# A graph network layer on one core: programs of their own for the closing steps, the final pair's gates as plain products, its mixing on VectorE

## The reference

```
mask   = (adj[None] == labels)                       # 4 labels
weight = mask / (sum(mask, -1) + EPS)
agg    = einsum('dbmn,bnh->bmdh', weight, hid)       # mean over neighbours, per label
out    = relu(agg @ Wd.T + bd)
r = sigmoid(out @ Wri.T + bri + hid @ Wrh.T + brh)
z = sigmoid(out @ Wzi.T + bzi + hid @ Wzh.T + bzh)
n = tanh(out @ Wni.T + bni + r * (hid @ Wnh.T + bnh))
out = (1 - z) * n + z * hid
out = (out - mean(out)) / sqrt(var(out) + LN_EPS) * gamma + beta
```

## Time and profile before

| what | value |
|---|---|
| median of 3 runs | 548.65 us (547.62 to 548.74) |
| the profiled execution | 547.88 us, of which the span from first to last instruction 546.1 us |
| PE busy | 512.1 us, 94% of the span |
| PEld busy | 467.4 us, 86% |
| DVE busy | 436.0 us, 80% |
| ACT busy | 387.9 us, 71% |
| POOL busy | 301.4 us, 55% |
| mean granted clock of TensorE | 0.976 of 2.4 GHz |

### The profile page before, as it was taken

How to read it: one execution, slowest core, us unless ns; L and a number is a source line. 1 busy time by engine, 2 the same in 40 slices (tenths; PEclk the granted TensorE clock), 3 DMA queues, 4 the chain that set the end, 5 groups by cost and what they waited for, 6 DMA issues and landing times.

```text
span 546.1 us, 10515 instructions
## 1 busy us (share of the span) xinstructions
PE 512.1 (94%) x3011; PEld 467.4 (86%) x3011; DVE 436.0 (80%) x1075; ACT 387.9 (71%) x725; POOL 301.4 (55%) x311
## 2 busy tenths in 40 slices
PE   4759999999999999999999999999999999999970
PEld 2548999999999999999999999999999999999860
DVE  5685688888888888888888888888888888888755
ACT  4366777777777777777777777777777777777651
POOL 5564555655565556556655566565555665653333
PEclk9688999999999999999999999999999999999996
DMA  8302022122111221222111211121112122110100
GB/s 283 111 30 68 1 68 69 49 69 68 68 50 39 67 67 48 67 67 67 51 36 67 67 48 67 67 67 56 35 63 67 49 66 67 38 38 29 40 31 38
DMA packets 19877, 33.42 MB, mean 61 GB/s; under 512 B 2224, under 2 KB 6576, under 8 KB 19856
## 3 DMA queue, kind: packets, MB, share of 16 engines
q1 hardware_dynamic: 19728, 32.78, 18.4%
q0 software_dynamic: 128, 0.39, 0.2%
HBM read 24.77 MB, written 8.39 MB: 61 GB/s over the span
## 4 chain that ended last, share of the span: by engine, by line
PE 88%; issue 3%; POOL 3%; DVE 3%; ACT 2%; DMA 1%; SPq 0%; POOLq 0%; DVEq 0%; ACTq 0%
PE y_bank L281 33%; PE alpha L281 23%; PE gamma L281 11%; PE p_bank L344 11%; PE beta L281 6%; PE t_bank L383 2%; DMA shared<-in_wdT 1%; PE t_bank L325 1%; DVE masks L645 1%; DVE y_lo L592 0%; POOL shared L840 0%; POOL shared L845 0%; POOL x_lo L827 0%; ACT y_hi L448 0%; ACT x_hi L495 0%
## 5 line engine op out<-in xcount | busy, mean ns | idle before, releaser
L827 POOL TENSOR_TENSOR x_lo<-x_f,x_hi 128x1024 fp32r<-128x1024 f32 x31 | 80.9, 2611 | 102.0 <-ACT x_hi L495 102.0
L448 ACT ACTIVATE y_hi<-y_bank 128x512 fp32r<-128x512 f32 x128 | 76.8, 600 | 63.7 <-PE y_bank L281 63.6
L281 PE MATMUL y_bank<-wd_hi,x_hi 128*128 128x512 f32 x256 | 106.1, 414 | 4.7 <-DVE wd_lo L580 4.7
L281 PE MATMUL y_bank<-wd_lo,x_hi 128*128 128x512 f32 x256 | 103.6, 405 | 0.0
L281 PE MATMUL y_bank<-wd_hi,x_lo 128*128 128x512 f32 x256 | 103.1, 403 | 0.0
L592 DVE TENSOR_TENSOR y_lo<-y_bank,y_hi 128x512 fp32r<-128x512 f32 x128 | 86.9, 679 | 13.9 <-ACT y_hi L448 13.8
L344 PE MATMUL p_bank<-y_hi,masks 128*128 128x256 f32 x256 | 68.0, 287 | 9.6 <-DVE y_lo L592 8.6
L864 POOL TENSOR_TENSOR o_lo<-o_sums,o_hi 128x512 fp32r<-128x512 f32 x32 | 41.4, 1295 | 52.8 <-ACT o_hi L547 52.8
L344 PE MATMUL p_bank<-y_lo,masks 128*128 128x256 f32 x256 | 67.6, 286 | 0.0
L456 ACT ACTIVATE p_bank<-p_bank,ratio 128x256 f32<-128x256 f32 x128 | 52.5, 456 | 11.0 <-PE p_bank L344 11.0
L281 PEld LDWEIGHTS y_bank<-wd_hi,x_hi 128*128 128x128 f32 x256 | 49.9, 195 | 12.0 <-issue 5.5
(11 more groups left out here) (116 smaller groups left out, 1357.2 us busy)
## 6 DMA issues: line engine op xcount, KB each, us to landing
x_f<-in_xT SPq DMA_DIRECT2D x32, 256.0 KB, 2.6
x_rows<-in_x SPq DMA_DIRECT2D x32, 256.0 KB, 3.0
out<-shared SPq DMA_DIRECT2D x32, 256.0 KB, 2.0
adj_in<-in_adjT SPq DMA_DIRECT2D x31, 128.0 KB, 2.4
shared<-in_wgT SPq DMA_DIRECT2D x2, 576.0 KB, 7.4
shared<-in_wdT SPq DMA_DIRECT2D x3, 256.0 KB, 6.4
vec_rows<-in_vectors SPq DMA_DIRECT2D x1, 512.0 KB, 8.4
x_rows<-in_vectors SPq DMA_DIRECT2D x1, 512.0 KB, 10.0
```

Of the source, the lines that this page charges most:

```text
L281: done = nc.tensor.matmul(dst, m, w, start=(first and t == 0), stop=(last and t == 2), skip_group_check=inside)
L448: nc.scalar.activation(y_hi[:, g, half(b)], y_bank[b][:, :], ACT.Copy)\
L827: nc.gpsimd.tensor_tensor(*split_lo(x_lo[:, k % XRING, :, :], x_f[:, k % 2, :, :], x_hi[:, k % XRING, :, :])).then_inc(xlo_ready, 1)
```

## The change

The steps 32 to 35 are replaced by a function `tail()` on each engine, written out for pairs 29 to 31 (`run_steps` now ends before step 32).

- The final pair's gates are eight plain products (no sums of `x` or `o`): each of four banks (`y_bank0`, `y_bank1`, `p_bank`, `beta`) collects one 128-node by two-gate block of one graph; ACT writes the bias into it first (`seed`), the `x` halves come early and the `o` halves when `o_lo` is there. The graph with index 1 (`ODD`) comes first.
- Its sigmoids are taken bank by bank, its hidden part and sum in pieces of 128 columns, its mixing `x - n`, `z *`, `+ n` on DVE for each graph, its statistics and normalization for each graph with stores of their own.
- Pair 30 keeps the seven products; pairs 29 and 30 are normalized by ACT (scaling with `rstd`) and POOL (addition of beta) in place of DVE. On SP the store of pair 30 stands ahead of the two stores of pair 31.
- PE's transposes of pair 31 come after the product S2,T2 in place of before it; the relu of `o` is done once for the whole bank.
- The plain products need block `B12` of the weights, split in step 3, and a bias `half_bias`, made on POOL in step 3. `n_sb` lies elsewhere in `shared`, so that `B12` stays whole until then.

The parts of the diff in the steps, whole:

```
-WBLOCKS = 7
+WBLOCKS = 8
-ASKED = (B11, T1, T2, B21, T3, T4, B22)
+ASKED = (B11, T1, T2, B21, T3, T4, B22, B12)
-        n_sb = later(4608, 1)
+        n_sb = later(7168, 1)
-            for i in range(LAST, STEPS):
+            for i in range(LAST, PAIRS):
                 step(i, lambda n, k=1: n)
...
@@ ACT, after u3 and ahead of o_hi of the sums
                 if i == 2:
                     weights_o(B22)
+                if i == 3:
+                    weights_x(B12)
+                    weights_o(B12)
...
@@ POOL, after x_lo and ahead of the mixing
                 if i == 2:
                     for w in (B21, T3, T4, B22):
                         weights_o(w)
+                if i == 3:
+                    weights_o(B12)
+                    nc.gpsimd.tensor_tensor(half_bias[:, :], vec_rows[:, 0:512], bias_step[:, :], ALU.add)\
+                        .then_inc(half_bias_ready, 1)
                 if has_pair(m):
                     pool.wait_ge(tanh_ready, up(m + 1))
```

The tail programs, cut to their order:

```
+    # SP
+    def tail():
+        rows(PAIRS - 2)
+        sp.wait_ge(result_ready, 2 * (PAIRS - 3))
+        store(PAIRS - 4)
+        rows(PAIRS - 1)
+        sp.wait_ge(late_ready, 1)
+        store(PAIRS - 3)
+        sp.wait_ge(late_ready, 2)
+        store(PAIRS - 2)
+        for n, g in ((1, ODD), (2, EVEN)):
+            sp.wait_ge(end_ready, n)
+            sp.dma_start(out[PAIRS - 1][:, g * H:(g + 1) * H], end_out[:, g, :]).then_inc(stored[1], 16)
+    # PE (waits for operands left out)
+        product(alpha, A11, B11).then_inc(p1_done, 1)
+        (second label sums of graph 1)
+        product(gamma, S1, T1).then_inc(p5_done, 1)
+        product(alpha, S2, T2).then_inc(p6_done, 1)
+        (transposes)
+        product(beta, A12, B21).then_inc(p2_done, 1)
+        product(alpha, S3, T3).then_inc(p7_done, 1)
+        from_x((ODD, 0))
+        product(alpha, A22, T4).then_inc(p4_done, 1)
+        from_x((ODD, 1))
+        product(gamma, S4, B22).then_inc(p3_done, 1)
+        from_o((ODD, 0))
+        from_x((EVEN, 0))
+        from_o((ODD, 1))
+        from_x((EVEN, 1)).then_inc(x_gates_done, 1)
+        from_o((EVEN, 0))
+        pe.wait_ge(end_nh_ready, 1)
+        from_o((EVEN, 1))
+    # ACT, from the sigmoid of pair 30
+        sigmoid(last - 1)
+        end_gate((ODD, 0), end_r_ready)
+        end_gate((ODD, 1), end_z_ready)
+        tanh(last - 1)
+        scale_norm(last - 2, 0)
+        end_tanh(ODD, 2)
+        act.wait_ge(x_gates_done, 1)
+        nc.scalar.activation(end_nh[:, :], beta[:, 0:128], ACT.Copy).then_inc(end_nh_ready, 1)
+        end_gate((EVEN, 0), end_r_ready)
+        end_tanh(EVEN, 4)
+        end_gate((EVEN, 1), end_z_ready)
+        scale_norm(last - 1, 2)
+    # DVE, from the c12 sum of pair 30
+        moments(last - 2)
+        hidden(last - 1, gamma)
+        centre(last - 2, 0)
+        centre(last - 2, 1)
+        end_hidden(ODD, 0, 1, y_bank[0][:, 0:128])
+        end_sum(ODD, 0, 1)
+        end_hidden(ODD, 1, 1, y_bank[1][:, 0:128])
+        end_sum(ODD, 1, 2)
+        end_hidden(EVEN, 0, 2, p_bank[:, 0:128])
+        end_sum(EVEN, 0, 3)
+        end_hidden(EVEN, 1, 2, end_nh[:, :])
+        end_mixed(ODD, 1)
+        end_sum(EVEN, 1, 4)
+        end_moments(ODD, 1)
+        mixed(last - 1)
+        end_mixed(EVEN, 2)
+        end_centre(ODD, 1)
+        end_moments(EVEN, 2)
+        end_normal(ODD, 1)
+        moments(last - 1)
+        end_centre(EVEN, 2)
+        end_normal(EVEN, 2)
+        centre(last - 1, 0)
+        centre(last - 1, 1)
+    # POOL
+        mixing(last - 2)
+        root(last - 2)
+        mixing(last - 1)
+        add_beta(last - 2, 1)
+        end_root(ODD, 1)
+        end_root(EVEN, 2)
+        root(last - 1)
+        add_beta(last - 1, 2)
```

More of the change, by code:

```diff
@@ L17 @@
 LAST = FIRST + ROUNDS * BODY
+ODD, EVEN = 1, 0
 GATE = 3 * 128
@@ L100, in gnn_kernel @@
         normed = later(6144, 2).rearrange("p (k g f) -> p k g f", k=2, g=2)
+        sides = lambda t: t.rearrange("p (g f) -> p g f", g=2)
+        scratch = x_f[:, :, :, :].rearrange("p k b n -> p (k b n)")
+        end_rz = scratch[:, 0:1024].rearrange("p (g j f) -> p g j f", g=2, j=2)
+        end_pre = sides(scratch[:, 1024:1536])
+        end_out = sides(scratch[:, 1536:2048])
+        end_rn = out_rows
+        end_part = sides(o_sums[:, 0:4, :].rearrange("p b n -> p (b n)"))
+        end_stats = sb("end_stats", [128, 2, 6])
+        end_mv = sb("end_mv", [128, 2, 2])
+        end_rstd = sb("end_rstd", [128, 2])
+        end_nh = sb("end_nh", [128, 128])
+        half_bias = sb("half_bias", [128, 512])
         more_vec = x_rows[:, :, :, :].rearrange("p k g f -> p (k g f)")
@@ L111, in gnn_kernel @@
         mix = bank("mix")
+        gate_bank = {(ODD, 0): y_bank[0], (ODD, 1): y_bank[1], (EVEN, 0): p_bank, (EVEN, 1): beta}
+        end_n, end_d, end_mix = sides(alpha[:, :]), sides(gamma[:, :]), sides(t_bank[:, :])
         x_loaded = [sem("x_loaded0"), sem("x_loaded1")]
@@ L192, in gnn_kernel @@
         scaled_ready = sem("scaled_ready")
+        half_bias_ready = sem("half_bias_ready")
+        seeded = {key: sem(f"seeded_{key[0]}{key[1]}") for key in gate_bank}
+        gates_done = {key: sem(f"gates_done_{key[0]}{key[1]}") for key in gate_bank}
+        x_gates_done = sem("x_gates_done")
+        end_nh_ready = sem("end_nh_ready")
+        end_r_ready = sem("end_r_ready")
+        end_z_ready = sem("end_z_ready")
+        end_rn_ready = sem("end_rn_ready")
+        end_pre_ready = sem("end_pre_ready")
+        end_n_ready = sem("end_n_ready")
+        end_d_ready = sem("end_d_ready")
+        end_part_ready = sem("end_part_ready")
+        end_mix_ready = sem("end_mix_ready")
+        end_stats_ready = sem("end_stats_ready")
+        end_mv_ready = sem("end_mv_ready")
+        end_ve_ready = sem("end_ve_ready")
+        end_rstd_ready = sem("end_rstd_ready")
+        end_centred = sem("end_centred")
+        end_ready = sem("end_ready")
+        late_scaled = sem("late_scaled")
+        late_ready = sem("late_ready")
         result_ready = sem("result_ready")
@@ L269, in step, with rows, store @@
                         .then_inc(stored[j % 2], 16)
+            def rows(k):
+                sp.wait_ge(from_ready, k - 1)
+                sp.dma_start(x_rows[:, k % 2, :, :], x[k].rearrange("p (g f) -> p g f", g=2))\
+                    .then_inc(rows_loaded[k % 2], 16)
+            def store(j):
+                sp.dma_start(out[j].rearrange("p (g f) -> p g f", g=2), normed[:, j % 2, :, :]).then_inc(stored[j % 2], 16)
+            def tail():
[10 more added lines that the diff above has]
+                    sp.dma_start(out[PAIRS - 1][:, g * H:(g + 1) * H], end_out[:, g, :]).then_inc(stored[1], 16)
             run_steps(sp, step)
-            for slot in range(2):
-                sp.wait_ge(stored[slot], 16 * PAIRS // 2)
+            tail()
+            sp.wait_ge(stored[0], 16 * PAIRS // 2)
+            sp.wait_ge(stored[1], 16 * PAIRS // 2 + 16)
         @block.tensor
@@ L409, in step, with tail, product, from_x @@
                     count(i + 1)
+            def tail():
+                q, last, slot = PAIRS - 2, PAIRS - 1, (PAIRS - 1) % XRING
+                def product(dst, left, w):
+                    three_passes(dst[:, 0:GATE], x_hi[:, q % XRING, left, :], x_lo[:, q % XRING, left, :],
+                                 wx_hi[:, w, :], wx_lo[:, w, :])
+                    return three_passes(dst[:, 128:512], o_hi[:, q % 2, left - 1, :], o_lo[:, q % 2, left - 1, :],
+                                        wo_hi[:, w, :], wo_lo[:, w, :])
+                inner = {(ODD, 0): ((A11, B11), (A12, B21)), (ODD, 1): ((A11, B12), (A12, B22)),
+                         (EVEN, 0): ((A21, B11), (A22, B21)), (EVEN, 1): ((A21, B12), (A22, B22))}
+                o_place = {A21: 3, A22: 0, A11: 1, A12: 2}
+                def from_x(key):
+                    pe.wait_ge(seeded[key], 1)
+                    for left, w in inner[key]:
+                        done = three_passes(gate_bank[key][:, 0:GATE], x_hi[:, slot, left, :], x_lo[:, slot, left, :],
+                                            wx_hi[:, w, :], wx_lo[:, w, :])
+                    return done
+                def from_o(key):
+                    for left, w in inner[key]:
+                        at = o_place[left]
+                        done = three_passes(gate_bank[key][:, 128:512], o_hi[:, last % 2, at, :],
+                                            o_lo[:, last % 2, at, :], wo_hi[:, w, :], wo_lo[:, w, :])
+                    done.then_inc(gates_done[key], 1)
+                pe.wait_ge(alpha_loaded, PAIRS - 1)
+                pe.wait_ge(olo_ready, PAIRS - 1)
+                product(alpha, A11, B11).then_inc(p1_done, 1)
+                pe.wait_ge(p_scaled, 4 * PAIRS)
+                for b in range(2):
+                    d = 2 * b + 1
+                    for part in (y_hi, y_lo):
```

(31 more changed lines are left out.)

207 lines of the change are left out of this document (added).

## The result

The changed kernel takes 554.45 us (median of 4 runs, 553.79 to 555.07) against 548.65 before: ratio 1.011, 95% interval 1.0092 to 1.0128. Forecast were 553.6 and 551.2 to 555.7. The profiled execution has a span of 552.0 us.

A forecast was written before the change was run, and what follows sets the result against it. PE was taken as the bound except at the two ends, where any delay from step 3 on is paid in full; front 8.9 less tail 3.9 gave +5.0, on the median 553.6 us, range 551.2 to 555.7.

The forecast's parts named there:

- The front's order: Step 3: POOL waits 4.6 us for ACT's wo_hi ahead of the mixing, which starts 6.94 late.
- From DVE to PE: Step 3: DVE's late mix add delays c22, PE idles 6.0 us; y_lo then makes the P matmuls 7.0 late.
- The clock: After the 6.0 us gap PE returns at granted clock 0.50, making the next product 8.9 us late, not 7.0.
- The tail: Closing steps: the new order ends the program 3.9 us earlier, bounds 2.5 to 4.9.
- The walk itself: Step-by-step timing of the tail: c12 of pair 30 at 522.3, DVE ending at 536.65, the span at 542.2.
- The named weakness: Tail: SP stores pair 30 first, so ACT's scalings (0.81) and POOL's addition (1.3) precede the three stores.
- The clock did not stay high: Rival, 10%: the clock stays high after PE's gap; front 7.0, tail 3.9, so +3.1, 551.8 us.
- The front was not hidden: Rival, 6%: POOL's wait in step 3 costs nothing and only the tail's gain is left, 544.7 us.
- The tail did not give nothing: Rival, 5%: DVE's smaller pieces and pair 30 stored first cancel the tail's gain; 8.9 alone, 557.5 us.
- A stall of some 3.9: Rival, 2%: a partly hidden stall of about 3.9 us would give no change.

The follow-up runs named there:

- e1: The changed kernel with POOL's split of B12 and half_bias moved from ahead of the mixing to behind rstd in step 3: 545.67 us, ratio 0.9954.
- e4: The changed kernel with ACT's two splits of B12 moved up to the start of step 3, POOL's order kept: 549.40 us, ratio 1.0029.
- e3: The changed kernel with 30 matmuls of zeros on PE in step 3, between A22,T4 and the wait for c22: 553.11 us, ratio 1.009.
- e5: e1 with POOL's addition of beta for pair 29 moved behind the root of the odd graph in the tail: 545.46 us, ratio 0.9939.
- e6: e5 with pair 30's moments, centrings and root ahead of the last pair's closing operations, and its store last: 542.82 us, ratio 0.9892.
- e7: e6 with DVE's split of B12 moved from ahead of the c22 sum to the end of step 3: 542.87 us, ratio 0.99.
- e8: The changed kernel with POOL's o_lo of step 3 made to wait for DVE's mix add of pair 0: 554.81 us, ratio 1.012.
- e2: The kernel before with only the change's step 3 insertions (B12 split, half_bias, unread) and the old closing steps: 557.41 us, ratio 1.016.

## Why the prediction was right, point by point

**The front's order: right.** POOL's wait was 4.66 (forecast 4.6), its releaser ACT's wo_hi; the mixing started 6.9 late (73.79, against 67.61 less the head's 0.71). e1 and e4 show that both the wait and the 2.3 us of work behind it count.

**From DVE to PE: one term missing.** The sum had the mix add at 0.70. It took 1.74 beside POOL's o_lo, and PE's gap was 6.9 where 6.0 were forecast. The step that failed is "z_part comes 6.9 late, and the rest follows with the durations of before": POOL's o_lo came late as well and landed on the add.

**The clock: the mechanism right, its size too large.** PE came back at 0.50. The low clock lasted 4.6 us after the return (79.89 to about 84.5), not the 5.8 of the earlier trace rows, and cost 1.2 us (e3) where 1.9 stood in the sum (8.9 less 7.0). The two errors, +1.04 and -0.7, nearly cancel: forecast 8.9, measured 9.2. That the front fits is partly luck.

**The tail: right in kind, 1.3 us too good.** 2.6 where 3.9 were forecast. Of the missing, 0.92 is the product of end_nh, 1.20 in place of 0.28 (e5 gives 0.84 of it back); the sigmoid of pair 30 starts 0.54 after the c12 sum ends (530.75 to 531.29), where the sum had nearly nothing. The walk itself held: the c12 sum ends at 530.75, forecast 522.3 plus the shift of 8.48, 530.8; from DVE's last operation to the end 5.46, forecast 5.55. The last matmul ends 3.2 sooner on the shifted scale (537.9 less 8.48, against 532.6), not 4: PE's wait for end_nh was 1.30 where the sum had 0.7, off the deciding path as forecast. The named weakness, pair 30's store ahead of the last pair's, is real: e6 takes 2.0 us out of it.

**The total.** By the traces both ends together are +6.6 (9.19 less 2.58) where +5.0 stood in the sum, and nearly all of the difference is the tail's. The profile's head was 0.71 shorter by chance, and the medians differ by 5.8. The forecast of 553.6 is 0.85 below the 554.45 measured, inside the stated range.

**The rivals.** The clock did not stay high. The front was not hidden. The tail did not give nothing. A stall of some 3.9 did not occur: PE's gap was 6.90.

## What to carry to other kernels

An insertion into an in-order engine costs what stands behind it, not its busy time: 2.3 us of work with a wait of 4.7 ahead of a chain that had no slack cost PE 9 us once, and the same work behind that chain under 1. Before placing a one-time preparation, look for the instruction that another engine already waits for and go behind it. Then look what the work pushes back in turn: an operation that moves in time can land beside one of another engine that it slows (e7, e8). In a closing sequence, let the engine that runs without a gap finish last, with the shortest path from it to the store.

## What the runs showed of the hardware

DVE's TENSOR_TENSOR operations whose two inputs both lie in SBUF stood still while a POOL instruction that had started first ran: 1.74 us in place of 0.70 beside 1.26 of POOL, 1.20 in place of 0.28, 1.31 in place of 0.54. Operations with one input in PSUM did not (in e5 the sum of o_sums and alpha at 535.00 took 0.43 in the middle of POOL's addition of beta, 534.75 to 536.01). Taking the overlap away restored both durations (e5, e8). The Trainium skill, SBUF — State Buffer, section "Who interferes with whom", says that a DVE instruction with two SBUF inputs contends with a GpSimd instruction that reads SBUF; the trace agrees, with the numbers above. It goes the other way too: POOL's addition of one column, which started just behind DVE's mix add (540.78 and 540.62), took 0.59 us, and 0.19 where no such operation ran; the mix add kept its 0.70.

Two inputs in SBUF are not the only case. The masks of e7 have one, and four of them took 1.71 beside POOL in place of 0.90. And the trace of the kernel before had the effect already, in a small operation. The ratios of the counts (L621, 128x4, both inputs in SBUF) took (shortest, median and longest, in ns):

```profile
L621 DVE TENSOR_TENSOR ratio<-rcount,counts x32: 158/626/689, 13.9 to 496.6; 128x4 f32<-128x4 f32 x32
```

In the timeline the 27 that run beside a POOL instruction take 0.52 to 0.69 us, the other five 0.16. So the trace of before already showed that such an operation waits for POOL; the sum did not ask what the late o_lo would run beside.

PE came back at half clock after 2.33 us of idle (e4), and in e2 fell behind waits of under 1 us that left it up in the profile of before. I had counted on short gaps being free of this; they are not reliably so, and the old closing steps, with two such waits of PE, were exposed to it.
